# First layer's cross attention: where the products for the maxima stand in TensorE's queue

## The reference

```python
q = (xq @ Wq).reshape(B, N, HEADS, D_HEAD)
k = (xc @ Wk).reshape(B, S, HEADS, D_HEAD)
v = (xc @ Wv).reshape(B, S, HEADS, D_HEAD)
scores = jnp.einsum('bnhd,bshd->bhns', q, k) * scale
attn = jax.nn.softmax(scores, axis=-1)
out = jnp.einsum('bhns,bshd->bnhd', attn, v).reshape(B, N, HEADS * D_HEAD)
return out @ Wo + bo
```

## Time and profile before

| | |
|---|---|
| median of three runs | 3550.25 us (3549.68 to 3553.19) |
| the profiled execution, its own time | 3553.4 us |
| its span, first to last instruction | 3551.6 us |
| granted TensorE clock, mean | 0.94 of full |
| busy: PE, DVE, ACT, POOL | 91%, 64%, 51%, 31% of the span |

### The profile page before, as it was taken

One profiled execution on the slowest core, in us unless ns is written; L12 is line 12 of the kernel. 1 busy time (PEld: TensorE's weight loads), 2 busy tenths in 40 slices (PEclk: granted clock), 3 DMA queues, 4 the chain that ended last, 5 costly groups with the idle time before them and its releaser, 6 DMA issues. The chain is left out here.

```text
span 3551.6 us, 49453 instructions
## 1 busy us (share of the span) xinstructions
PE 3225.4 (91%) x17084; PEld 1849.4 (52%) x17084; DVE 2257.8 (64%) x4094; ACT 1828.3 (51%) x3365; POOL 1084.1 (31%) x537
## 2 busy tenths in 40 slices
PE   6969996899979999999999779989699699999969
PEld 4734443688844444444444357743377444444347
DVE  4437774444356666666666445579566599999634
ACT  3424543344524444444444434448556278888844
POOL 1026664000037777777777700002100000000000
PEclk8969998999979999999999889979899789999989
DMA  5788884899985666666666052244544622332131
GB/s 200 275 206 214 229 224 170 305 339 317 324 192 135 150 157 155 144 144 144 145 157 156 35 206 101 83 132 144 196 154 170 215 87 85 111 99 89 57 130 54
DMA packets 367019, 588.63 MB, mean 166 GB/s; under 512 B 47056, under 2 KB 197120, under 8 KB 365640
## 3 DMA queue, kind: packets, MB, share of 16 engines
q1 hardware_dynamic: 361614, 582.41, 55.3%
q10 hardware_dynamic: 5178, 3.31, 0.4%
HBM read 344.19 MB, written 241.29 MB: 165 GB/s over the span
## 5 line engine op out<-in xcount | busy, mean ns | idle before, releaser
L2084 ACT ACTIVATE a_prob<-a_ring 128x512 f32<-128x512 f32 (+1 forms) x1088 | 575.5, 601 | 657.1 <-PE a_ring L1989 584.8
L2110 DVE TENSOR_REDUCE a_blk_max<-a_ring 128x1 f32<-128x402 f32 x1024 | 519.4, 567 | 323.6 <-PE a_ring L1973 323.5
L1666 ACT ACTIVATE a_prob<-a_ring 128x512 f32<-128x512 f32 (+1 forms) x1088 | 582.3, 605 | 168.6 <-PE a_ring L1591 164.6
L1939 POOL TENSOR_TENSOR a_prob_sum<-a_prob,a_prob_sum 128x1024 f32<-128x1024 f32 x256 | 599.3, 2377 | 3.0 <-ACT a_prob L2084 3.0
L2011 PE MATMUL a_pv<-a_prob,a_v 128*64 128x512 f32 (+1 forms) x2176 | 536.9, 612 | 0.0
L1711 DVE TENSOR_REDUCE a_blk_max<-a_ring 128x1 f32<-128x402 f32 x1024 | 507.0, 566 | 35.0 <-PE a_ring L1578 27.9
L1988 PE MATMUL a_ring<-a_q_stack,a_k_stack 128*128 128x512 f32 (+1 forms) x1088 | 464.1, 427 | 14.8 <-DMA a_q_second<-maxima 12.7
L1989 PE MATMUL a_ring<-a_q_second,a_k_second 65*128 65x512 f32 (+1 forms) x1088 | 435.6, 400 | 0.0
L1939 POOL TENSOR_TENSOR a_prob_sum<-a_prob 128x1024 f32<-128x1024 f32 x128 | 302.0, 2370 | 419.9 <-DVE a_chunk_sum L2141 244.5
L1609 PE MATMUL a_pv<-a_prob,a_v 128*32 128x256 f32 (+2 forms) x4096 | 341.1, 406 | 13.5 <-ACT a_prob L1666 7.8
L1578 PE MATMUL a_ring<-a_k_stack,a_q_stack 63*128 63x402 f32 (+1 forms) x1280 | 285.0, 425 | 34.5 <-DMA a_q_stack<-q_lo_cross 17.4
(11 more groups left out here) (276 smaller groups left out, 4693.3 us busy)
## 6 DMA issues: line engine op xcount, KB each, us to landing
a_k_stack<-k_hi_cross SPq DMA_DIRECT2D x96, 400.5 KB, 4.2
a_v<-v_cross SPq DMA_DIRECT2D x48, 768.0 KB
a_k_stack<-k_lo_cross SPq DMA_DIRECT2D x80, 400.5 KB, 4.2
a_k_second<-k_hi_cross SPq DMA_DIRECT2D x32, 801.0 KB, 12.5
v_cross<-p_v_sb SPq DMA_DIRECT2D x48, 512.0 KB, 3.4
k_hi_cross<-p_split_hi SPq DMA_DIRECT2D x120, 200.0 KB, 2.7
k_lo_cross<-p_split_lo SPq DMA_DIRECT2D x120, 200.0 KB, 2.9
a_q_stack<-q_hi_self SPq DMA_DIRECT2D x64, 256.0 KB, 4.1
```

What stands on the lines that cost most here:

```text
L1666: nc.scalar.activation(prob[0:keys, tau % RC, m, :], ring[0:keys, score_place(e) % BANKS, :], ACT.Exp, scale=a.scale).then_inc(exp_done, 1)
L1939: nc.gpsimd.tensor_tensor(prob_sum[:, h], prob_of(i * NCP + cp, h), other, ALU.add)\
L2084: nc.scalar.activation(prob_of(w, h)[0:keys, ch % 2, :], ring[0:keys, score_bank(e), :], ACT.Exp, scale=a.scale).then_inc(exp_done, 1)
L2110: nc.vector.reduce_max(dst, ring[:, max_bank(g), 0:a.blk], AX.X).then_inc(item_read, 1)
```

## The change

`cut` returns, for a cross attention, the number of pairs given out by the unit before. TensorE's loop and VectorE's loop, which both use it, are the same text as before.

```diff
     def cut(w):
 
 
-        return max(pairs_by(w - 1), pairs_by(w) - 2) if a.cross else pairs_by(w)
+        return pairs_by(w - 1) if a.cross else pairs_by(w)
 
```

## The result

The changed kernel takes 3567.08 us (median of 9 runs, 3564.64 to 3578.35) against 3552.92 for the kernel before on the same chips (9 runs, 3549.68 to 3560.88). The ratio is 1.0044 with a 95% interval of 1.0033 to 1.0056: 14 us slower, clear of noise. 3569.4 was predicted, with a range of 3561 to 3578.

What follows compares the result with a forecast made beforehand. TensorE was taken to bound the first layer's cross attention. 60 three-pair units at 0.28 us (16.8) plus 2.3 for the ramp gave +19.1 us, 3569.4 us after allowing for the median 3.15 below the profiled execution; range 3561 to 3578.

Steps and rivals of the forecast that it cites:

- What bounds the phase, and that nothing else moves: First layer's cross attention: TensorE sets the pace, its matmul row busy 800.00 of 800.00 us; all other phases as before.
- The covers counted at nothing: VectorE's late steps, last_sum and other work around the burst of reads stay hidden; cover 0.63 us in a fifth unit.
- One block less, 0.19 us: Three-pair units: no separate block of max products between scores and values, 0.19 us shorter if nothing waits.
- S1's wait, +0.17 us: Next unit's first score product waits for its bank: due 0.76 us behind the first max product, open at 1.12.
- S2 to S4, +0.11 us: Next unit's second to fourth score products wait for reads of max products: 0.09, 0.01 and 0.01 us lost.
- The ramp, +2.3 us: Units w=1 and w=2: bursts of ten and eight max products delay later scores, together +2.3 us, uncertain by half a microsecond.
- The term for w=2: Burst of eight max products: the next unit's fourth score product needs the sixth read, about 3.73 us with its load; +1.1 us.
- that for w=1: Burst of ten max products: the fourth score product of w=2 needs the eighth read; +1.2 us.
- The sum: Whole kernel: 16.8 us for 60 three-pair units and 2.3 us for the ramp, +19.1 us.
- The rule against the row: Weight loads on TensorE: rows show a wait holding up the load; the skill's reorder window pulls loads ahead of matmuls in flight.
- The second rival: Only the next unit's first score product waits, the other three's loads run ahead: some 12.3 us slower, 3562.5; chance 0.17.

Runs made afterwards that it cites:

- e4: The changed cut with VectorE reading only 64 of the 402 columns of each max product, against the kernel before: 3539.89 us, ratio 0.9961.
- e3: The old cut with VectorE reading only 64 of the 402 columns of each max product, against the kernel before: 3546.06 us, ratio 0.9989.
- e5: Old cut, one unit with four max pairs in place of two with three, against the kernel before: 3548.08 against 3551.30 us, ratio 0.9987.
- e7: The changed cut in unit w=2 alone (eight max products in one burst), otherwise the kernel before: 3555.58 us, one run.
- e6: The changed cut in unit w=1 alone (ten max products in one burst), otherwise the kernel before: 3550.94 us, one run.
- e8: Three-pair units from w=4 on with all three max pairs ahead of the values, ramp as before, against the kernel before: 3572.98 us, ratio 1.0077.

## Why the prediction was right

- **What bounds the phase, and that nothing else moves.** Right. Each unit without three pairs kept its length to some hundredths, but for those behind a three-pair unit, and neither ScalarE, GpSimd nor a DMA came into a wait of TensorE. The covers counted at nothing held: last_sum follows the six reads (1860.29) and is over at 1861.50, ahead of the next unit's first read at 1862.47.
- **One block less, 0.19 us.** Right: in e4 against e3 a three-pair unit is 0.19 us shorter in the median, 10.75 us over the 60 steady ones; e5 gives 6.17 for 29 blocks, 0.21 each.
- **S1's wait, +0.17 us.** Right: first and fifth units are 0.16 us longer in the median (60 of them, 9.9 us in all).
- **S2 to S4, +0.11 us.** Wrong in size: the units behind lost 0.045 and 0.033 in the median, 2.5 us in all instead of 6.6. The step that failed is "the load takes 0.19 of that, so 0.04 us is spare". In the changed kernel S2's load starts at 1858.49 and its matmul at 1858.57, while the load still runs for 0.1 us. For the loads of S2 to S4 behind the 60 changed units that distance is 0.08 to 0.11 us, 0.09 in the median, so the spare is about 0.14 of the 0.22 to 0.23 us. The loads came as late as predicted (S2's 0.48 behind S1's, 0.14 later than before), but S2's matmul was not delayed and S4's by 0.03 us. A changed unit cost 0.21 us, not 0.28: 12.65 against 16.8.
- **The ramp, +2.3 us.** Too small: 5.96. The term for w=2 held (1.14 in e7; its 3.73 us for the sixth read is 3.71 by the prediction's own rows, which leaves it at 1.1); that for w=1 left out that the clock would fall behind it (4.78 in e6).
- **The sum.** 19.1 us were predicted, the phase lost 18.6. The two errors (4.2 too much, 3.7 too little) cancel: that the sum came closer than its terms is luck, since the fall of the clock was not foreseen. The medians differ by 14.2, the spans by 14.5. That the predicted 3569.4 lies only 2.3 us from the measured 3567.08 is partly luck too: it was counted from 3550.25, and the kernel before measured 3552.92 beside the changed one. In the profiled execution of the changed kernel the scores of w=0 came 2.9 us earlier than before, and what follows w=223 was 1.3 us shorter, both outside the edit; 18.6 lies inside what the interval allows (11.7 to 19.9 us).
- **The rule against the row.** The second rival's result of 0.17 us a unit is near the measured 0.21, but not by its mechanism. All four loads waited for a read (rows above), so the window of the Trainium skill, "TensorE: Matmul & The Clock Gate", section on what happens when a matmul is issued, pulled none past its semaphore. What came true is another statement of that page of the Trainium skill: in its section on the clock gate it says that a matmul can begin before the load of its weights is complete, and the 0.08 us at 1858.49 and 1858.57 agree.

## What to carry to other kernels

Moving work behind a longer piece can save the cost of a separate block, but where products share a ring of buffers, ask first who empties it: count from the first product when each read is over, and set it beside the place in the queue that needs the buffer. An early part between two products of the pacing engine may look like a needless interruption and be the time in which the slower reader catches up. The cheaper gain was to have fewer blocks with the same reads under cover (e5), not to join them into a burst.

## What the runs showed of the hardware that was not expected

- A score matmul's row began 0.08 to 0.11 us behind the start of its own weight load of 0.19 us where the load had waited for a read and the row of the product ahead still ran (S2 to S4); without a wait the distance was 0.22 to 0.23.
- TensorE gave up the full clock behind a burst of ten products that began 0.2 us after the clock had risen and whose last four came one read at a time, over 1.9 us (busy 3.60 of 4 us in that window). It had the clock back about 7 us later, and the ramp lost 3.6 us more than counted without this. The 60 waits of 0.29 us in the steady units left the clock at 1.00, and so did the burst of eight in w=2 alone. Whether it is the number of single reads or the place right behind the rise that tells them apart was not tried.
- The last max product of a block, where it waited for its bank, cost 0.1 us more than its wait: its weight load did not run under another product (e8).
